# Windowed-attention block with MLP on one core: first norm and its turning moved into the preceding MLP phase through device memory, second norm on DVE as eight tensor-scalar operations

## The reference

```
xs  = roll(x, (-4, -4), axis=(1, 2));  win = 8x8 windows of xs, 64 tokens each
h   = layernorm(win) * ln1_g + ln1_b
q, k, v = h @ wq + bq, h @ wk + bk, h @ wv + bv          # 3 heads of 32
attn = softmax(q k^T / sqrt(32));  o = attn @ v
win = win + o @ wo + bo
h2  = layernorm(win) * ln2_g + ln2_b
win = win + gelu(h2 @ w1 + b1) @ w2 + b2                 # 96 -> 384 -> 96
out = windows put back, rolled by (+4, +4)
```

## Time and profile before

| | us |
|---|---|
| median of 3 runs | 5121.04 |
| the runs | 5121.0, 5121.04, 5125.81 |
| span of the profiled execution | 5118.4 |
| what lies around the span, against the lowest run | 2.6 |

### The profile page before, as it was taken

The page is one execution under the profiler, slowest core; times in us unless marked ns, Lnnn a source line. Parts: engine busy times, 40 slices in busy tenths (PEclk is TensorE's granted clock), DMA queues, the critical chain, the costliest instruction groups (busy, mean ns, idle before and its releaser), DMA issues.

```text
span 5118.4 us, 275139 instructions
## 1 busy us (share of the span) xinstructions
PE 4931.8 (96%) x103124; PEld 4154.1 (81%) x103124; DVE 4072.6 (80%) x9254; ACT 3873.0 (76%) x8206; POOL 3623.5 (71%) x3589
## 2 busy tenths in 40 slices
PE   7999999999999999999999999999999999999999
PEld 6888888888888888888888888887888888888887
DVE  8969778697786977869788796887968879698786
ACT  7859688595886958769587695976949769496794
POOL 6868667686676866767767677676776767777676
PEclk9999999999999999999999999999999999999999
DMA  3141331313213132131322314223042230422304
GB/s 109 34 119 54 94 94 42 116 48 102 86 48 116 42 111 77 56 113 37 117 74 62 112 33 123 68 68 109 26 123 68 74 108 24 124 65 77 108 26 122
DMA packets 222028, 410.68 MB, mean 80 GB/s; under 512 B 29225, under 2 KB 131850, under 8 KB 221898
## 3 DMA queue, kind: packets, MB, share of 16 engines
q1 hardware_dynamic: 220336, 409.06, 27.0%
q10 hardware_dynamic: 1562, 0.50, 0.0%
HBM read 208.11 MB, written 201.33 MB: 80 GB/s over the span
## 4 chain that ended last, share of the span: by engine, by line
PE 55%; DVE 16%; DMA 9%; issue 8%; SPq 7%; ACT 2%; DVEq 2%; POOL 1%; ACTq 0%; POOLq 0%
PE psum L576 12%; PE psum L702 6%; PE psum L591 6%; PE psum L622 6%; PE psum L651 5%; PE psum L608 5%; PE psum L688 5%; PE psum L637 5%; DMA oT<-turned_rows 5%; DMA turned_rows<-normed 4%; SPq L269 4%; PE psum L544 4%; DVE normed L1002 3%; SPq L275 2%; DVE normed L1009 2%
## 5 line engine op out<-in xcount | busy, mean ns | idle before, releaser
L340 POOL TENSOR_TENSOR probs<-probs,prob_inv 128x512 f32<-128x512 f32 x771 | 783.1, 1043 | 839.6 <-DVE prob_inv L982 836.2
L988 DVE TENSOR_TENSOR stream<-stream,psum 128x384 f32 (+1 forms) x1024 | 547.1, 549 | 298.5 <-PE psum L702 225.0
L750 ACT ACTIVATE normed<-stream,shift,rstd 128x96 f32 (+1 forms) x2072 | 770.5, 461 | 17.8 <-issue 16.1
L902 DVE BATCH_NORM_STATS2 stats<-stream 128x6 f32 (+2 forms) x4224 | 721.3, 243 | 58.0 <-DVE stream L988 29.4
L379 POOL TENSOR_TENSOR rstd<-variance,minus_half 128x8 f32<-128x8 f32 (+2 forms) x201 | 745.0, 3707 | 15.7
L347 POOL TENSOR_TENSOR hT<-hT_upper,hT_lower 96x1024 f32<-96x1024 f32 x258 | 614.2, 2380 | 11.8 <-DVE hT_lower L951 6.8
L702 PEld LDWEIGHTS psum<-w_w,gelu_odd 128*64 128x64 f32 x12288 | 512.4, 137 | 59.4 <-issue 59.4
L974 DVE TENSOR_REDUCE prob_sum<-probs 128x8 f32<-128x512 f32 x771 | 492.5, 678 | 84.2 <-ACT probs L784 84.1
L966 DVE TENSOR_TENSOR probs<-psum,row_max 128x512 f32<-128x512 f32 x771 | 533.2, 692 | 26.6
L830 ACT ACTIVATE gelu_odd<-psum 128x512 f32<-128x512 f32 x768 | 418.7, 593 | 174.8 <-PE psum L688 156.5
L702 PE MATMUL psum<-w_w,gelu_odd 128*64 128x96 f32 x12288 | 536.4, 247 | 12.2 <-ACT gelu_odd L830 12.2
(11 more groups left out here) (94 smaller groups left out, 11327.9 us busy)
## 6 DMA issues: line engine op xcount, KB each, us to landing
turned_rows<-normed SPq DMA_DIRECT2D x624, 128.0 KB
stream<-in_x SPq DMA_DIRECT2D x272, 192.0 KB
out<-stream SPq DMA_DIRECT2D x256, 192.0 KB
stream<-in_x SPq DMA_DIRECT2D x272, 180.0 KB
out<-stream SPq DMA_DIRECT2D x256, 180.0 KB
probsT<-turned_rows SPq DMA_DIRECT2D x112, 384.0 KB, 3.2
oT<-turned_rows SPq DMA_DIRECT2D x112, 384.0 KB, 3.2
turned_rows<-gelu_odd SPq DMA_DIRECT2D x144, 128.0 KB
```

What stands on the lines that cost most here:

```text
L340: nc.gpsimd.tensor_tensor(block_h, block_h, inv, ALU.mult).then_inc(probs_ready, 1)
L750: last = nc.scalar.activation(normed1[:, t, :], stream[:, slot, t * C:(t + 1) * C], ACT.Identity, bias=shift1[:, index, t:t + 1], scale=rs ...
L902: last = nc.vector.bn_stats(stats[:, index, c, :], stream[:, slot, c * C:(c + 1) * C])
L988: nc.vector.tensor_tensor(part, part, psum[:, banks[g], 0:GROUP], ALU.add).then_inc(added, 1)
```

## The change

- ACT no longer norms unit u+3 in attention step u. The first norm of a unit of the next batch runs on ACT in the MLP phase, one unit in each MLP step j of 2 to 13 behind the gelus of unit j+1, and one more behind the gelus of unit 14; the first three units of a batch are normed in attention steps 8, 10 and 12. In the first batch each attention step norms one unit, as before.
- DVE turns the normed tile by a block transpose (`turn_h1`), which lands in a buffer in the unused second half of `probs` (MLP phase) or in `gelu_even` (attention). PE's eight transposes, their PSUM banks and the semaphores around them are gone.
- SP sends the turned tile to a new device memory ring of 32 slots in one transfer (`send_h1`), and fetches it in attention step s for unit s+3 in three transfers (`fetch_h1`) into one of two `h_raw` tiles. The fetch waits for the v projection two units back. The loads of the next batch move from a block of their own into the attention steps, one unit in each, behind the fetch.
- ACT copies `h_raw` to `hT_upper` from SBUF, after it has copied all four q and k parts and ahead of the v copies; POOL subtracts for `hT_lower` in two halves behind its probabilities. DVE's subtraction and POOL's addition into `hT` are gone. The v projection reads `h_raw` directly, in products of 32 output rows where they had 64, so 64 instructions where there were 32. The q and k copies of ACT write a permuted layout.
- The second norm on DVE is eight tensor-scalar operations of 128x96 (subtract, multiply) with no wait between, in place of two operations of 128x768.
- Statistics of the first norm are finished on POOL two units at a time in place of four.

The core of the diff:

```diff
+            def send_h1(u, source):
+
+                wait_apart(sp, h1_turned, u + 1)
+                slot = u % SLOTS if isinstance(u, int) else u & (SLOTS - 1)
+                sp.dma_start(turned1_dram[slot].rearrange("b p x -> p b x"),
+                             source.rearrange("p (b x) -> p b x", b=CBLOCKS)).then_inc(h1_left, 16)
+
...
+            def fetch_h1(u, parity):
+
+                if not (isinstance(u, int) and u < 2):
+                    wait_apart(sp, v_done, 2 * (u - 1))
+                wait_apart(sp, h1_left, 16 * (u + 1))
+                slot = u % SLOTS if isinstance(u, int) else u & (SLOTS - 1)
+                for cb in range(CBLOCKS):
+                    sp.dma_start(h_raw[parity][BLOCK * cb:BLOCK * (cb + 1), :].rearrange("c (t x) -> c t x", t=TBLOCKS),
+                                 turned1_dram[slot, cb].rearrange("(t c) x -> c t x", c=BLOCK))\
+                        .then_inc(h1_back[parity], 16)
...
+            def mlp_traffic(batch_row):
                 batch = 2 * batch_row
-                for n in range(2):
-                    send_turned(batch + n, turned_early, n)
-                    fetch_turned(batch + n, raw_early[n], n)
-                send_turned(batch + 2, turned_early, 2)
-                wait_apart(sp, pv_done, batch + BATCH)
+                wait_apart(sp, v_done, 2 * (batch + BATCH + 2))
                 fetch_turned(batch + 2, raw_late[0], 2)
                 send_turned(batch + 3, turned_late, 3)
                 fetch_late(batch + 3, 3)
...
+                for i in range(BATCH - 4):
+                    n = i % RING
+                    send_turned(batch + i + 4, turned_late, n)
+                    store(batch_row + i // 2, i % 2)
+                    if i >= 2:
+                        send_h1(batch + BATCH + i + 1, turned1_late)
+                    fetch_late(batch + i + 4, n)
+                for i in range(BATCH - 4, BATCH):
+                    if i < BATCH - 1:
+                        send_h1(batch + BATCH + i + 1, turned1_late)
+                    store(batch_row + i // 2, i % 2)
 
                 wait_apart(sp, stored, 16 * sum(LOAD_DMAS) * (batch_row + BATCH_ROWS))
...
+            with sp.Fori(1, BATCHES) as b:
+                batch_row = b * BATCH_ROWS
+                batch = b * BATCH
+                for s in range(BATCH):
+                    if s in (10, 12, 14):
+                        send_h1(batch + BATCH + (s - 10) // 2, turned1_early)
+                    fetch_h1(batch + s + 3, (s + 3) % 2)
+                    row = batch_row + BATCH_ROWS + s // 2
+                    load(row, row & (WROWS - 1), s % 2)
+                    if s in (6, 9, 11):
+                        n = (6, 9, 11).index(s)
+                        send_turned(batch + n, turned_early, n)
+                    if s in (7, 10):
+                        n = (7, 10).index(s)
+                        fetch_turned(batch + n, raw_early[n], n)
+                mlp_traffic(batch_row)
...
+            def copy_hT_lower(u, parity):
+
+                upper, lower = [half[0:C, :] for half in hT_split]
+                for g in range(2):
+                    tokens = slice(g * SHARES, (g + 1) * SHARES)
+                    pool.wait_ge(hT_upper_copied, 2 * u + g + 1)
+                    nc.gpsimd.tensor_tensor(lower[:, tokens], h_raw[parity][0:C, tokens], upper[:, tokens],
+                                            ALU.subtract).then_inc(hT_copied, 1)
...
+            def project_v(u, parity):
+                pe.wait_ge(h1_back[parity], 8 * CBLOCKS * (u - parity) + 16 * CBLOCKS)
...
-                            last = nc.tensor.matmul(
-                                psum[WT * side:WT * (side + 1), V_BANKS[g], t * C:(t + 1) * C],
-                                hT[:, tokens], qkv_w[:, 2, :], start=True, stop=True)
+                            for part in range(2):
+                                at = part * SHARES + (2 * (4 * g + t) + side) * BLOCK
+                                keys = WT * side + BLOCK * part
+                                last = nc.tensor.matmul(
+                                    psum[keys:keys + BLOCK, V_BANKS[g], t * C:(t + 1) * C],
+                                    h_raw[parity][:, at:at + BLOCK], qkv_w[:, 2, :], start=True, stop=True)
                     last.then_inc(v_done, 1)
...
+            def copy_hT_upper(u, parity):
+
+                act.wait_ge(h1_back[parity], 8 * CBLOCKS * (u - parity) + 16 * CBLOCKS)
+                if not (isinstance(u, int) and u == 0):
+                    act.wait_ge(qk_done, 4 * u)
+                for g in range(2):
+                    tokens = slice(g * SHARES, (g + 1) * SHARES)
+                    nc.scalar.activation(hT_split[0][0:C, tokens], h_raw[parity][0:C, tokens], ACT.Copy)\
+                        .then_inc(hT_upper_copied, 1)
...
                     copy_qk(front, 2)
-                for g in range(2):
-                    copy_hT_upper(u + 3, g)
+                    copy_qk(front, 3)
+                copy_hT_upper(u + 3, 1 - half)
                 if not absent(front):
                     copy_v(front, half, 0)
                     copy_v(front, half, 1)
-                    copy_qk(front, 3)
...
+                def mlp_step(j, odd):
+                    gelus(batch + j, odd, 1)
+                    copy_h2T_upper(batch + j + 2, odd)
+                    gelus(batch + j + 1, 1 - odd, 0)
+
...
-                        copy_h2T_upper(batch + j + 2, odd)
-                        gelus(batch + j + 1, 1 - odd, 0)
+                        mlp_step(j, odd)
+                        normalise1(batch + BATCH + j + 1, j + 1)
                 gelus(batch + BATCH - 2, 0, 1)
+                normalise1(batch + 2 * BATCH - 1, BATCH - 1)
                 gelus(batch + BATCH - 1, 1, 0)
                 gelus(batch + BATCH - 1, 1, 1)
 
...
+            def turn_h1(u, turned):
+                if not (isinstance(u, int) and u == 0):
+                    wait_apart(dve, h1_left, 16 * u)
+                dve.wait_ge(ln1_ready, u + 1)
+                nc.vector.transpose(
+                    turned.rearrange("p (b w t r) -> p t b w r", b=CBLOCKS, t=TILES, r=4),
+                    normed1[:, :, :].rearrange("p t (b w r) -> p t b w r", b=CBLOCKS, r=4)).then_inc(h1_turned, 1)
...
-                dve.wait_ge(centre2_step, (BATCH - AHEAD) * b + index - AHEAD + 1)
-                nc.vector.tensor_tensor(normed2[:, :, :], normed2[:, :, :],
-                                        rstd2[:, index, :].unsqueeze(2).to_broadcast((P, TILES, C)),
-                                        ALU.mult).then_inc(ln2_ready, 1)
+                for t in range(TILES):
+                    last = nc.vector.tensor_scalar(
+                        normed2[:, t, :], stream[:, slot_of(u), t * C:(t + 1) * C],
+                        mean2[:, index, t:t + 1], rstd2[:, index, t:t + 1], ALU.subtract, ALU.mult)
+                last.then_inc(ln2_ready, 1)
 
             def turn_h2(u, turned, first):
 
@@ -1042,37 +1089,30 @@
                     for h in range(HEADS):
                         sums(middle, 1 - half, h)
...
-                def mlp_step(j, parity, row, half):
+                def mlp_step(j, parity, row, half, turns):
                     normalise2(batch + j + 3, j + 3)
-                    scale2(b, batch + j + 3, j + 3)
                     turn_h2(batch + j + 3, turned_late, False)
+                    if turns:
+                        turn_h1(batch + BATCH + j, turned1_late)
                     statistics1(batch + BATCH + AHEAD + j, AHEAD + j, batch_row + BATCH_ROWS + row, half)
                     copy_h2T_lower(b, j + 2, parity)
                     add_mlp(batch + j)
 
```

355 lines of the change are left out of this document (169 added, 186 removed).

## The result

| | before | after |
|---|---|---|
| median of 4 runs | 5121.51 | 5463.52 (5458.86 to 5473.51) |
| ratio, 95% interval | | 1.067 (1.065 to 1.068) |
| span of the profiled execution | 5118.4 | 5458.5 |
| until the first gelu table load | 224.5 | 251.7 |
| attention phase, mean of the 15 behind the first MLP phase | 180.6 | 186.1 |

What follows compares the result with a forecast made beforehand. Attention was taken as bound by PE and ACT, both near full, steps closing through a loop across both. 5121 + 59 (attention steps) + 39 (turns) + 77 (MLP) + 20 (start) = 5316; own range 5220 to 5400, overall range 5060 to 5450.

Steps and rivals of the forecast that it cites:

- Start, +20: Kernel start: first units go once more through device memory, about 9, plus DVE work in the first batch; +20 (0 to 35).
- Attention steps, +59: Attention steps: 11.26 against 11.03, through a longer ACT loop ahead of the first v copy; +0.23 in 256 steps, +59.
- the 5.73 from scores to oT: Attention step: time from PE's start of scores to ACT's start of the oT copy, taken as 5.73.
- the restart: Attention step: from PE's resumed loads after a late v copy to the next scores; 0.77 to 1.15.
- case C: Rival, the small cases: no restart loss in attention steps (+8), MLP chain within its slack (0); 5188, chance 0.19.
- 64 products of 32 rows: v projection on PE in attention: 1.37 if they cost what 32 products do, 2.74 otherwise; the first was taken.
- Turn of the phases, +39: First attention step of a batch: fetch behind SP's wait for all stores, ACT waits 2.6; fifteen turns, +39 (25 to 55).
- MLP, +77: MLP phase: chain over three units late by 1.3, 0.43 a unit, taken as 0.3; 16 units, 16 phases, +77.
- the gain of 0.84: DVE's second norm in the MLP phase: eight operations of 96 columns take 1.33 in place of 2.17.
- The send ahead of the fetch: SP in the MLP phase, odd units: send_h1 before the fetch costs one issue of 0.6 and 0.5 to 1 of passage.
- Rival B: Contention: DVE's norms meet POOL's operations more often, 2 us more in a chain of three units; 5487, chance 0.10.
- What would show it: Signs: attention phases 185 to 188, PE idle about 1 a step, ACT's step 0 wait, MLP phases near 141, operations 160 to 250 ns.

Runs made afterwards that it cites:

- the three edits: Changed kernel with v copies first on ACT, POOL's last hT_lower of a phase later, SP's wait for the stores behind the first fetch: 5263.7.

## Why the prediction was wrong, point by point

- **Direction:** right. Slower was given 0.77. The terms other than the MLP's came to 110 where 118 was forecast, but by luck: the attention steps were too high by 64 and the turns too low by 49.
- **Start, +20:** measured 27.
- **Attention steps, +59 (bounds 8 and 105):** measured about -5, outside its bounds. The chain closes as written, and PE's wait of about 1 is 1.02. Three terms were off and partly cancel: the 5.73 from scores to oT, which I held fixed, is 5.43 (-0.30), the restart is 0.83 where I took 0.96 (-0.13), and the stretch from oT to the restart is 4.77 where I had 4.56 (+0.21). The case C had the restart. The v copies moved ahead gave 174 us, so what stands ahead of v in this chain was the thing to read.
- **64 products of 32 rows:** 1.46 from start to start, near the 1.37 that I took. That also agrees with the Trainium skill (TensorEngine Tiling (Array Packing), Theoretical Speedup).
- **Turn of the phases, +39:** measured 88, 5.9 in each of fifteen. The place was right, and so was the wait for the stores. At the first turn, where SP's loop does not go back, the step grew by 2.2, where I had 2.6. At the fourteen others it grew by 6.1: SP stands 2.4 to 2.8 behind its loop's branch, a term that I did not have, ACT waits about 4.2 in place of 2.6, and TensorE is at its lower level behind the standstill, which I had not priced either.
- **MLP, +77 (bounds 0 and +170):** measured 230, beyond its bound. This is the step that failed. I took one unit of the middle of a phase and asked how late a chain of three units becomes. First, eight operations were to gain 0.84 (1.33 in place of 2.17). Without POOL they take 2.00, and 3.4 on the mean where two took 2.8; in the kernel before they cost 5.7 a phase. Second, the beginning of the phase was not looked at. There POOL's run had been made longer by the change's own subtraction, and the first turning is 5.2 later; 4.2 a phase. I had put that subtraction at nothing on POOL's busy time of a whole phase. Third, the 2.9 us of norm between gelus. I charged it with 1.57 in three units (2.9 less the slack of 1.33), 8 a phase, of which the gain of 0.84 was to take half; with its turning it cost 3.1 a phase, so this term was too large. The send ahead of the fetch, charged with some 1.2 in every other unit, nearly half of the term, has no more than a share of the 1.4 a phase left over; no run shows the 0.5 to 1 that I put for its passage.
- **Rival B** had the time, 5487, and the chance of 0.10; that its 2 us in a chain of three units comes so near is partly luck, since it had no term for the start of the phase. Its mechanism, DVE's norm against POOL, is the largest part (4.2 of the 14.4 by a run of the changed kernel, 5.7 by one of the kernel before). Its wording, that each of eight operations has a chance to lose, is borne out: a norm of eight has twice the stretched operations of a norm of two, and with the three edits the seventh operation of a phase's first norm lost 2.8, once POOL's next operation came sooner. How much one loses follows how long POOL runs without a gap: eight took 9.27 and two 7.49 in the same place, and 3.8 both, once POOL's run was broken. The rule of the Trainium skill (SBUF — State Buffer, Who interferes with whom) on the shared port pair agrees with these rows also for tensor-scalar operations, if they ran in the two-port mode, which no row shows: one of 0.32 stands for up to 4.91. I had quoted the rule, and given it a tenth.
- **What would show it:** attention phases of 185 to 188 (186.1), PE idle about 1 a step for v (1.02), the wait in step 0 alone: all came. The MLP phases near 141 and operations of 160 to 250 ns did not (150.1; 320 ns long, 240 apart).
